# Latent attention: the units of the maximum pass end in step 18, and the maxima are turned ahead of the value group of step 20

## The chip, the cores and the metric

The program runs on one core of one Trainium2 chip. The metric is the device time of one execution in microseconds. Three runs of the kernel before are shown below; the profile is of one further execution.

## The reference, cut to what matters

Two layers of cross attention and feed-forward work on x (8 batches of 100 tokens, 256 wide). The change touches the attention of the second layer, which attends to a context of 1444 positions, 64 wide, for 16 heads:

```
scores = jnp.einsum('bhsr,bhlr->bhsl', q_r, k_r)
attn = jax.nn.softmax(scores, axis=-1)
ctx_c = jnp.einsum('bhsl,bld->bhsd', attn, kv_r)
ctx_lat = jnp.einsum('bhsd,hkd->bhsk', ctx_c, w_kc_kv)
x = x + jnp.tanh(g_xattn[1]) * (ctx_lat @ Wo.T)
```

The softmax subtracts the maximum over the 1444 positions from each row of scores. The kernel gets these maxima in a pass of its own, one batch ahead.

## The kernel before, in words

All of the attention of the second layer runs in one stage (ST_XB), with the order of the work written out by hand for each engine. For each of 8 batches there are 24 steps (SP_): 2 groups of 8 heads times 12 tiles of 121 context positions. The loops of TensorE, VectorE (DVE), ScalarE (ACT) and GpSimd (POOL) all count the same steps; semaphores hold them together.

In step s TensorE computes the scores of one tile: two matmuls with the high parts (L1748) and two with the low parts (L1751), 400 columns each. The second pair has 66 rows: 64 of the low part of the keys, and two rows of ones against which qm2 holds the negated maxima, as a high and a low part. So the maximum is subtracted inside the matmul, and scores(b, 0) waits until the DMA has written the maxima rows (semaphore qm). There are two pairs of PSUM banks for scores: step n waits for the exponential of step n - 2. ScalarE takes the exponential (L891) into a ring of 12 tiles, prob.

Every six steps (s % 6 == 2) TensorE does a value group (L1766): the values of six tiles times prob, accumulated in bank 7. The groups of batch b in steps 8, 14, 20 and in step 2 of the next batch; the one of step 20 reads steps 12 to 17 and needs nothing newer.

Between scores TensorE does the units of the maximum pass for batch b + 1 (queries_keys, L1730 and L1731): 39 units, 13 blocks of 128 rows by 3 segments of about 482 keys. VectorE takes the maximum of each unit out of PSUM (L1219). The table UNITS says how many units are done before step s. Units, the sums of probabilities (L1775), the projection (L1784) and the turned maxima share three banks in rotation (next_slot): a use waits until the third use before it has been emptied.

When the 39 units are done, VectorE reduces them to the negated maxima nmx (L1224, negative_maxima), TensorE turns nmx (L1737, maxima_turned), VectorE copies its high part nmh and low part nml out of PSUM (L1232, L1234, maxima_rows), and SyncE issues four DMAs (L447, L448) that write them into the two rows of qm2 for the next batch. On TensorE this turn is the last thing of step 20, behind the value group. On VectorE step 20 holds, in this order, the addition add_probabilities (L1242), negative_maxima and maxima_rows:

```
if s in (8, KT + 8) and b < B:
    add_probabilities(2 * b + s // KT, 8)
...
if s == 20 and more:
    negative_maxima(b + 1, k)
    maxima_rows(b + 1)
```

VectorE does more in these steps: four reciprocals of the sums (L1256, steps 16 to 19, behind the maxima of the step), the normalising of the context (L1261, step 19), in steps 0 and 1 of the next batch the last additions of the sums (L1247, L1251; the latter waits for the GpSimd addition of step 22), in step 2 the low parts of the next keys (low_keys, L1212, three of them), for which units of step 3 wait, and from step 3 again maxima. GpSimd adds the other tiles of probabilities (L658, L661) and rotates the keys of the batch after the next (L610, L612, L615).

slot_sums works out from UNITS at which use of the rotating banks the sums lie, so it follows the table.

Of the kernel before, what the change touches and what calls it, by code (L numbers as in the profile page):

```python
# [18 lines left out]
def flamingo(nc, a, out, scratch, sorted_x, sorted_y):  # L19
# [41 lines left out]
    with ctx:  # L61
# [216 lines left out]
        def end_stage(eng, turn):  # L278

            eng.drain().then_inc(stage, 1)  # L280
            eng.wait_ge(stage, turn * ENG)
# [12 lines left out]

        SP_ = 2 * KT
        NU = 3 * MT
        UNITS = (0, 0, 0, 0, 2, 4, 6, 8, 11, 14, 16, 18, 21, 24, 26, 29, 30, 32, 34, 36, 39, 39, 39, 39, 39)
        ADDS = (1, 1, 2, None, 3, 4, 5, None, 6, 7, 8, None)

        def key_rows(t):  # L300
# [6 lines left out]
        def slot_sums(i):  # L307

            p, late = (i + 1) // 2, i % 2 == 0
            first = NU + 1 + (0 if p == 0 else NU + 2 + (p - 1) * (NU + 4) - (0 if p < B else NU + 1))  # L310
            units = UNITS[KT + 4 if late else 4] if p + 1 < B else 0
            return first + units + (2 if late and p >= 1 else 0)

        def unit_columns(m):
            return slice(m * P, m * P + P) if m < MT - 1 else slice(HQ - P, HQ)
# [679 lines left out]
        def _(dve):  # L995
# [219 lines left out]
            def maximum(u):  # L1215

                k, g, m = next(slot), u // MT, u % MT
                dve.wait_ge(xb["fill"], k + 1)
                dve.tensor_reduce(mx3[:, m, g:g + 1], PS[:, 4 + k % 3, 0:SEG[g][1]], AX.X, ALU.max).then_inc(xb["free"], 1)  # L1219
                return next(freed)  # L1220
# [59 lines left out]
            for b in range(B + 1):  # L1280
                for s in range(SP_ if b < B else 11):
# [4 lines left out]
                    if more:  # L1286
                        for u in range(UNITS[s], UNITS[s + 1]):
                            k = maximum(u)
# [113 lines left out]
        def _(pe):  # L1402
# [306 lines left out]
            def next_slot(emptied_by):  # L1709

                k = len(held)
                if k >= 3:
                    pe.wait_ge(*held[k - 3])
                held.append(emptied_by)
                return 4 + k % 3
# [3 lines left out]
            def queries_keys(b, u):  # L1719

                g, m = u // MT, u % MT
                cols, keys = unit_columns(m), slice(SEG[g][0], SEG[g][0] + SEG[g][1])
                if m == 0:
                    pe.wait_ge(xb["kth"], 3 * b + g + 1)
                    pe.wait_ge(xb["kl"], 3 * b + g + 1)
                if u == 0:
                    pe.wait_ge(xb["one"], 1)
                    pe.wait_ge(xb["q2"], b + 1)
                bank = PS[:, next_slot((xb["free"], next(freed))), 0:SEG[g][1]]
                mm(bank, qs[:, b].rearrange("p h s -> p (h s)")[:, cols], kth[:, b % 2, keys], start=True, stop=False)  # L1730
                mm(bank, qm2[:, b % 2, cols], kl2[:, b % 2, keys], start=False, stop=True).then_inc(xb["fill"], 1)  # L1731

            def maxima_turned(b):

                k = next_slot((xb["free"], next(freed)))
                pe.wait_ge(xb["nmx"], b + 1)
                pe.transpose(PS[0:MT, k, 0:P], nmx[:], ident[:]).then_inc(xb["fill"], 1)  # L1737

            def scores(b, s):

                n, hp, t = b * SP_ + s, s // KT, s % KT
                keys = slice(t * KP, t * KP + key_rows(t))
                if s == 0:
                    pe.wait_ge(xb["qm"], 64 * (b + 1))
                if n >= 2:
                    pe.wait_ge(xb["ex"], n - 1)
                for g in range(2):
                    mm(PS[0:key_rows(t), 2 * (n % 2) + g, 0:GC], kth[:, b % 2, keys],  # L1748
                       qs[:, b, 8 * hp + 4 * g:8 * hp + 4 * g + 4].rearrange("p h s -> p (h s)"), start=True, stop=False)
                for g in range(2):  # L1750
                    last = mm(PS[0:key_rows(t), 2 * (n % 2) + g, 0:GC], kl2[:, b % 2, keys],  # L1751
                              qm2[:, b % 2, (2 * hp + g) * GC:(2 * hp + g + 1) * GC], start=False, stop=True)
                last.then_inc(xb["s"], 1)

            def values(c):

                b, i = c // 4, c // 2
                if c % 4 == 0:
                    pe.wait_ge(xb["nrot"], 3 * (b + 1))
                if c % 2 == 0 and i >= 1:  # L1760
                    pe.wait_ge(xb["raw"], i)
                pe.wait_ge(xb["ex"], 6 * c + 6)
                for n in range(6 * c, 6 * c + 6):
                    t = n % KT
                    for g in range(2):
                        last = mm(PS[g * DC:g * DC + DC, 7, 0:GC], kvn[0:key_rows(t), b % 2, t], prob[0:key_rows(t), n % RING, g],  # L1766
                                  start=(t == 0), stop=(t == KT - 1))
                last.then_inc(xb["pv"], 1)

            def probability_sums(i):  # L1770

                k = next_slot((xb["sums"], i + 1))
                pe.wait_ge(xb["ad"], 3 * i + 3)
                for g in range(2):
                    last = mm(PS[g * DC:g * DC + DC, k, 0:GC], ones[:], accd[:, g], start=True, stop=True)  # L1775
                last.then_inc(xb["fill"], 1)

            def project(b):

                k = next_slot((xb["free"], next(freed)))  # L1780
                pe.wait_ge(xb["cx"], 2 * b + 2)
                for c in range(NC):
                    for p in range(H1 // 2):
                        last = mm(PS[:, k, c * S:(c + 1) * S], w2p[:, p, c * P:(c + 1) * P], cx[:, p], start=(p == 0), stop=(p == H1 // 2 - 1))  # L1784
                last.then_inc(xb["fill"], 1)
# [3 lines left out]
            for b in range(B + 1):  # L1789
                for s in range(SP_ if b < B else 11):  # L1790
                    n, more = b * SP_ + s, b + 1 < B
                    if b < B:
                        scores(b, s)
                    if more:
                        for u in range(UNITS[s], UNITS[s + 1]):
                            queries_keys(b + 1, u)
                    if s % 6 == 2 and 8 <= n < B * SP_ + 3:
                        values((n - 8) // 6)
                    if s == 3 and b >= 1:
                        probability_sums(2 * b - 1)  # L1800
                    if s == KT + 3:
                        probability_sums(2 * b)
                    if s == 10 and b >= 1:
                        project(b - 1)
                    if s == 20 and more:
                        maxima_turned(b + 1)
            end_stage(pe, ST_XB)
            norm("n3", xT)
            end_stage(pe, ST_N3)
# [167 lines left out]
```

## Time and profile before

| | us |
|---|---|
| median of 3 runs | 1738.02 |
| the three runs | 1728.39, 1738.02, 1741.69 |
| the profiled execution | 1731.37 |
| its span | 1729.6 |
| TensorE (PE) busy | 1516.6 (88%) |
| VectorE (DVE) busy | 913.5 (53%) |
| ScalarE (ACT) busy | 592.5 (34%) |
| GpSimd (POOL) busy | 719.9 (42%) |
| mean granted TensorE clock | 0.92 |

The span is the time from the first to the last instruction of the profiled execution. The busy shares are means over all stages; the stage of the change takes some 500 us of the span, and what bounds it is to be read from its own stretches. A wait in brackets is the idle time of the engine ahead of an instruction and what ended it.

### The profile page before, as it was taken

Reading aid. Unit: us, or ns where it says so; the run is one execution under the profiler, and the core shown is the slowest. Engines: PE = TensorE matmul, PEld = TensorE weight load, DVE = VectorE, ACT = ScalarE, POOL = GpSimd, SP = SyncE. Lnnn points to the kernel's source line nnn. Section 1 sums busy time; section 2 is a strip of 40 time slices with the busy share of each in tenths; the row PEclk is TensorE's granted clock in tenths of the full one; section 3 lists DMA queues with packets and bytes.
Section 4 is the critical chain, followed back from the end, with each engine's and each line's share of the span. In section 5 each row is a group of like instructions: output and inputs, shape, how many; then the busy total and the mean of one; then the engine's idle time right before and its main releaser. Section 6 shows DMA issues by size and latency. Waiting matters only on the chain. (4 is left out here: it accounts for less than half of the span.)

```text
span 1729.6 us, 19632 instructions
## 1 busy us (share of the span) xinstructions
PE 1516.6 (88%) x6852; PEld 1060.0 (61%) x6852; DVE 913.5 (53%) x1402; ACT 592.5 (34%) x945; POOL 719.9 (42%) x509
## 2 busy tenths in 40 slices
PE   5897798899978999999999977789797978599998
PEld 3675465444446667666667643465555555499997
DVE  3744111356675766767767435745647272444454
ACT  2322121123323433433433433434434332234343
POOL 2731002046646786787876630423323131133231
PEclk8988898599997999999999998989899989699999
DMA  7004112610001101101100020000000000334441
GB/s 277 1 1 154 32 40 67 190 37 22 1 35 52 53 1 52 53 1 52 53 1 18 1 74 2 25 1 24 24 24 24 24 0 3 93 115 126 118 124 47
DMA packets 60297, 88.33 MB, mean 51 GB/s; under 512 B 7557, under 2 KB 44613, under 8 KB 60231
## 3 DMA queue, kind: packets, MB, share of 16 engines
q1 hardware_dynamic: 59206, 85.82, 15.7%
q0 software_dynamic: 1024, 1.64, 0.3%
q8 instruction: 40, 0.66, 0.2%
q14 instruction: 27, 0.21, 0.0%
HBM read 81.92 MB, written 5.41 MB: 50 GB/s over the span
## 5 line engine op out<-in xcount | busy, mean ns | idle before, releaser
L661 POOL TENSOR_TENSOR xc<-xc,prob 121x800 f32<-121x800 f32 x112 | 230.9, 2061 | 70.4 <-ACT prob L891 62.2
L891 ACT ACTIVATE prob<-PS 121x800 f32<-121x800 f32 x192 | 159.3, 838 | 269.2 <-PE PS L1751 266.4
L1219 DVE TENSOR_REDUCE mx<-PS 128x1 f32<-128x482 f32 (+1 forms) x312 | 185.5, 644 | 76.5 <-PE PS L1731 75.7
L585 POOL TENSOR_TENSOR e_wl<-e_wf,e_wh 128x768 fp32r<-128x768 f32 x33 | 70.9, 2148 | 200.8 <-ACT e_wh L815 159.3
L683 POOL TENSOR_TENSOR q<-q,qt 128x400 f32<-128x400 f32 x64 | 66.0, 1031 | 211.5 <-DVE qt L1338 211.5
L1766 PE MATMUL PS<-prob,kvn 121*64 121x400 f32 (+1 forms) x768 | 141.3, 518 | 0.9 <-ACT prob L891 0.9
L1748 PE MATMUL PS<-qs,kth 128*121 128x400 f32 (+1 forms) x384 | 117.4, 389 | 21.0 <-DMA qm<-nml 18.3
L1730 PE MATMUL PS<-kth,qs 128*128 128x482 f32 (+1 forms) x312 | 126.1, 404 | 7.6 <-DVE kl L1212 5.8
L1731 PE MATMUL PS<-kl,qm 66*128 66x482 f32 (+1 forms) x312 | 121.8, 390 | 0.0
L547 POOL TENSOR_TENSOR p<-d,sm 100x800 f32<-100x800 f32 x48 | 73.1, 1522 | 114.3 <-DVE sm L1041 114.3
L1751 PE MATMUL PS<-qm,kl 66*121 66x400 f32 (+1 forms) x384 | 109.6, 369 | 0.0
L1748 PEld LDWEIGHTS PS<-qs,kth 128*121 128x121 f32 (+1 forms) x384 | 69.2, 198 | 60.3 <-DMA qm<-nml 20.9
L1766 PEld LDWEIGHTS PS<-prob,kvn 121*64 121x64 f32 (+1 forms) x768 | 53.8, 141 | 76.9 <-issue 72.8
L1160 DVE TENSOR_TENSOR e_aw<-e_sg,PS 128x400 f32<-128x400 f32 x64 | 36.6, 571 | 116.3 <-ACT e_sg L821 116.3
L1836 PE MATMUL PS<-h,wq 128*128 128x400 f32 x256 | 92.4, 512 | 5.3 <-DVE q L1334 4.4
L1622 PE MATMUL PS<-e_hh,e_wh 128*128 128x400 f32 x264 | 93.2, 353 | 2.7 <-POOL e_wl L585 2.7
L1872 PE MATMUL PS<-o,wo 128*128 128x400 f32 x256 | 90.8, 511 | 3.7 <-ACT o L967 3.7
L1861 PE MATMUL PS<-pt,vg 100*128 100x400 f32 x128 | 55.6, 561 | 41.8 <-ACT pt L745 29.7
L1623 PE MATMUL PS<-e_hl,e_wh 128*128 128x400 f32 x264 | 92.0, 348 | 0.0
L1624 PE MATMUL PS<-e_hh,e_wl 128*128 128x400 f32 x264 | 91.7, 347 | 0.0
L739 ACT ACTIVATE d<-d 100x800 f32<-100x800 f32 x48 | 41.8, 870 | 134.2 <-DVE d L1033 134.2
L633 POOL TENSOR_TENSOR rr<-rp 96x400 f32<-96x400 f32 x32 | 32.9, 1027 | 117.1 <-DVE rp L1196 117.1
(248 smaller groups left out, 3178.0 us busy)
## 6 DMA issues: line engine op xcount, KB each, us to landing
e_wb<-routing SPq DMA_DIRECT2D x32, 400.0 KB, 3.9
wgu<-in_L_ffn_gate_up_proj SPq DMA_DIRECT2D x8, 1024.0 KB, 14.3
krt<-in_ctx_T SPq DMA_DIRECT2D x8, 722.0 KB, 4.2
ksw<-in_ctx_Tswap SPq DMA_DIRECT2D x8, 722.0 KB, 5.9
wdn<-in_L_ffn_down_proj SPq DMA_DIRECT2D x8, 512.0 KB, 8.6
wq<-in_L_ffn_Wq SPq DMA_DIRECT2D x4, 1024.0 KB, 5.2
wo<-in_L_ffn_Wo SPq DMA_DIRECT2D x4, 1024.0 KB, 5.4
e_wf<-in_L_ffn_Wg SPq DMA_DIRECT2D x32, 128.0 KB, 2.1
```

Of the source, the lines that this page charges most:

```text
L661: pool.tensor_tensor(accp, accp, prob[:, n % RING], ALU.add).then_inc(xb["ap"], 1)
L891: act.activation(prob[0:k, n % RING], PS[0:k, 2 * (n % 2):2 * (n % 2) + 2, 0:GC], ACT.Exp).then_inc(xb["ex"], 1)
L1219: dve.tensor_reduce(mx3[:, m, g:g + 1], PS[:, 4 + k % 3, 0:SEG[g][1]], AX.X, ALU.max).then_inc(xb["free"], 1)
L1622: mm(out_, wh, mh, start=start, stop=False)
L1623: mm(out_, wh, ml, start=False, stop=False)
L1624: return mm(out_, wl, mh, start=False, stop=stop)
L1730: mm(bank, qs[:, b].rearrange("p h s -> p (h s)")[:, cols], kth[:, b % 2, keys], start=True, stop=False)
L1731: mm(bank, qm2[:, b % 2, cols], kl2[:, b % 2, keys], start=False, stop=True).then_inc(xb["fill"], 1)
L1748: mm(PS[0:key_rows(t), 2 * (n % 2) + g, 0:GC], kth[:, b % 2, keys], qs[:, b, 8 * hp + 4 * g:8 * hp + 4 * g + 4].rearrange("p h s -> p (h s ...
L1751: last = mm(PS[0:key_rows(t), 2 * (n % 2) + g, 0:GC], kl2[:, b % 2, keys], qm2[:, b % 2, (2 * hp + g) * GC:(2 * hp + g + 1) * GC], start=F ...
L1766: last = mm(PS[g * DC:g * DC + DC, 7, 0:GC], kvn[0:key_rows(t), b % 2, t], prob[0:key_rows(t), n % RING, g], start=(t == 0), stop=(t == KT ...
L1836: last_ = mm(PS[:, QBANK[n], 0:HALF], wq2[:, c, (n % HG) * P:(n % HG + 1) * P], h1[:, c, half(n // HG)], start=(c == 0), stop=(c == NC - 1))
```

## The change

The table UNITS is another one: 27, 30, 31, 33, 36 and 39 units are done before steps 14 to 19, where 26, 29, 30, 32, 34 and 36 were; the last unit is in step 18 and not in step 19. The total stays 39. And on TensorE maxima_turned of step 20 stands ahead of the value group of that step. VectorE's order is left as it is, but for the maxima, which follow the table.

```
-        UNITS = (0, 0, 0, 0, 2, 4, 6, 8, 11, 14, 16, 18, 21, 24, 26, 29, 30, 32, 34, 36, 39, 39, 39, 39, 39)
+        UNITS = (0, 0, 0, 0, 2, 4, 6, 8, 11, 14, 16, 18, 21, 24, 27, 30, 31, 33, 36, 39, 39, 39, 39, 39, 39)
...
                     if more:
                         for u in range(UNITS[s], UNITS[s + 1]):
                             queries_keys(b + 1, u)
+                    if s == 20 and more:
+                        maxima_turned(b + 1)
                     if s % 6 == 2 and 8 <= n < B * SP_ + 3:
                         values((n - 8) // 6)
...
                     if s == 10 and b >= 1:
                         project(b - 1)
-                    if s == 20 and more:
-                        maxima_turned(b + 1)
```

## Rows read from the trace of the kernel before

**Rows 1.** The page: busy time of each engine, share, instructions.
```profile
PE 1516.6 (88%) x6852; PEld 1060.0 (61%) x6852; DVE 913.5 (53%) x1402; ACT 592.5 (34%) x945; POOL 719.9 (42%) x509
```

**Rows 2.** The view of the tile nml: who waited for it (us, times).
```profile
  PE PS L1748: 18.3, 8
```

**Rows 3.** Windows between two turns: us, busy time by engine, PEclk, DMA, GB/s.
```profile
577.68:642.06 64.38, 61.60 (x312) 43.69 (x313) 44.02 (x63) 25.02 (x32) 49.35 (x29) 0.95 0.11 36
...
897.84:960.40 62.56, 60.20 (x311) 43.17 (x312) 44.22 (x63) 25.04 (x32) 41.60 (x22) 0.97 0.05 13
```

**Rows 4.** Timeline of TensorE, first boundary: start, us, instruction, [idle before <-releaser].
```profile
571.48 0.39 PE L1730 MATMUL PS<-kth,qs 128*128 128x480 f32 x1
...
571.92 0.53 PE L1748 MATMUL PS<-qs,kth 128*121 128x400 f32 x2
...
572.75 4.25 PE L1766 MATMUL PS<-prob,kvn 121*64 121x400 f32 x24
577.68 0.27 PE L1737 MATMUL PS<-ident,nmx 128*13 128x128 f32 x1 [0.68 <-DVE nmx L1224]
...
582.53 1.02 PE L1748 MATMUL PS<-qs,kth 128*121 128x400 f32 x2 [1.93 <-DMA qm<-nml]
583.35 0.87 PE L1751 MATMUL PS<-qm,kl 66*121 66x400 f32 x2
```

**Rows 5.** Windows of 1 us, first boundary; the granted clock is third from the end.
```profile
583.00:584.00 1.00, 1.00 (x4) 0.96 (x4) 0.53 (x1) 0.00 (x0) 1.00 (x1) 0.50 0.00 0
...
588.00:589.00 1.00, 1.00 (x6) 0.37 (x4) 0.72 (x1) 1.00 (x2) 1.00 (x1) 0.56 0.00 0
```

**Rows 6.** Timeline of TensorE, third boundary.
```profile
711.53 0.85 PE L1748 MATMUL PS<-qs,kth 128*121 128x400 f32 x2 [1.93 <-DMA qm<-nml]
...
715.46 4.25 PE L1766 MATMUL PS<-prob,kvn 121*64 121x400 f32 x24
```

**Rows 7.** Timeline of VectorE, first boundary.
```profile
566.41 1.22 DVE L1219 TENSOR_REDUCE mx<-PS 128x1 f32<-128x480 f32 x2 [1.53 <-PE PS L1731]
...
575.44 1.99 DVE L1242 TENSOR_TENSOR xc<-prob 121x800 f32<-121x800 f32 x1
577.35 0.18 DVE L1224 TENSOR_REDUCE nmx<-mx 128x13 f32<-128x39 f32 x1
```

**Rows 8.** Timeline of ScalarE, first boundary: the exponentials of steps 21 and 22.
```profile
578.72 1.57 ACT L891 ACTIVATE prob<-PS 121x800 f32<-121x800 f32 x2 [5.03 <-PE PS L1751]
```

**Rows 9.** Timeline of TensorE, the first scores of batch 0.
```profile
521.82 1.02 PE L1748 MATMUL PS<-qs,kth 128*121 128x400 f32 x2 [4.75 <-DMA qm<-nml]
```

**Rows 10.** Timeline of GpSimd, first boundary: the additions of steps 21 and 22.
```profile
579.63 1.89 POOL L661 TENSOR_TENSOR xc<-xc,prob 121x800 f32<-121x800 f32 x1 [0.44 <-ACT prob L891]
...
582.64 2.64 POOL L661 TENSOR_TENSOR xc<-xc,prob 121x800 f32<-121x800 f32 x1
```

**Rows 11.** Timeline of VectorE, first and fourth boundary: last addition, low keys.
```profile
585.32 1.99 DVE L1251 TENSOR_TENSOR xc<-xc 121x800 f32<-121x800 f32 x1 [1.79 <-POOL xc L661]
...
779.47 5.22 DVE L1212 TENSOR_TENSOR kl<-krt,kth 64x482 fp32r<-64x482 f32 x3 [0.16 <-ACT kth L868]
```

**Rows 12.** Timeline of TensorE, first boundary: scores of step 3, first unit of step 4.
```profile
592.01 0.63 PE L1748 MATMUL PS<-qs,kth 128*121 128x400 f32 x2
...
595.45 0.39 PE L1730 MATMUL PS<-kth,qs 128*128 128x482 f32 x1
```

**Rows 13.** Timeline of TensorE, sixth and seventh boundary.
```profile
897.84 0.27 PE L1737 MATMUL PS<-ident,nmx 128*13 128x128 f32 x1 [0.67 <-DVE nmx L1224]
...
914.25 0.39 PE L1730 MATMUL PS<-kth,qs 128*128 128x482 f32 x1
...
955.91 4.25 PE L1766 MATMUL PS<-prob,kvn 121*64 121x400 f32 x24
...
974.51 0.62 PE L1748 MATMUL PS<-qs,kth 128*121 128x400 f32 x2
```

**Rows 14.** Timeline of VectorE: the addition L1251 of step 13, GpSimd idle.
```profile
622.19 0.98 DVE L1251 TENSOR_TENSOR xc<-xc 121x800 f32<-121x800 f32 x1
```

More of the change, by code:

```diff
@@ L296, in flamingo @@
         NU = 3 * MT
-        UNITS = (0, 0, 0, 0, 2, 4, 6, 8, 11, 14, 16, 18, 21, 24, 26, 29, 30, 32, 34, 36, 39, 39, 39, 39, 39)
+        UNITS = (0, 0, 0, 0, 2, 4, 6, 8, 11, 14, 16, 18, 21, 24, 27, 30, 31, 33, 36, 39, 39, 39, 39, 39, 39)
         ADDS = (1, 1, 2, None, 3, 4, 5, None, 6, 7, 8, None)
@@ L1796, in _ @@
                             queries_keys(b + 1, u)
+                    if s == 20 and more:
+                        maxima_turned(b + 1)
                     if s % 6 == 2 and 8 <= n < B * SP_ + 3:
@@ L1804, in _ @@
                         project(b - 1)
-                    if s == 20 and more:
-                        maxima_turned(b + 1)
             end_stage(pe, ST_XB)
```

## The prediction

> **What bounds the kernel.** I read the page first. TensorE is busy 88% of the span, no other engine more than 53% [rows 1]. Its costly groups send the reader to line 1748, the scores, whose idle time ends mostly with the copy of the maxima rows; the view of the tile nml puts that at 18.3 us in 8 waits, one for each batch [rows 2]. The windows between two turns of the maxima show what a batch costs: six of them, 62.6 to 64.6 us, the first 64.38 with TensorE busy 61.60 of them, the last 62.56 with 60.20 [rows 3]. So TensorE bounds this stage and every microsecond that it waits at a boundary between batches is a microsecond of the kernel. There are 7 boundaries that the edit touches (the eighth turn, of batch 0, is ahead of the loop).
>
> The timeline of TensorE at the first boundary shows what the reader has to see [rows 4]. The value group of step 20 starts at 572.75. The turn of the maxima comes behind it at 577.68, after 0.68 us of idle time that the negated maxima end. Steps 21 to 23 follow at once; then 1.93 us of idle time for the DMA, and the first scores of the new batch at 582.53. From there the matmuls take twice as long (0.87 for a pair instead of 0.53). The slices say why: the granted clock was 0.50, that is 1.2 GHz, from 583 us on, and back at 2.4 GHz within the slice from 588, some 6.4 us after work resumed [rows 5]. What went ahead was mostly idle time. At the third boundary it was back by the value group at 715.46, 3.9 us after work resumed at 711.53 [rows 6].
>
> **What decides is VectorE.** Its timeline at the first boundary has no gap from 566.41 to 577.53: nine maxima, four reciprocals, the normalising, the addition of probabilities (L1242, 1.99 us), and only then the 0.18 us reduction that makes nmx [rows 7]. The value group on TensorE lies exactly beside the tail of this. It is the cover of the wait that the edit uncovers.
>
> **The parts.**
> (a) Unit table: 39 units before and after, so no work is added. One unit (two matmuls, 0.44 us from the starts in [rows 4]) goes from step 19 to step 13, ahead of the value group of step 14; within steps 16 to 19 the rest is pushed forward. At step 20 TensorE arrives at the same time. VectorE has 8 maxima instead of 9 behind the value group of step 14 (one less, 0.57), but that value group ends 0.44 later, so nmx comes 0.13 us earlier. Bounds: 0.57 earlier, or 0.2 later (a bank not yet free). I take 0.13.
> (b) The turn moves ahead of the value group. TensorE reaches it at 572.75 instead of 577.0, and nmx is there at 577.40, plus the 0.15 us that passes in [rows 4, 7] between nmx and the turn: idle 4.8 us. Behind the waiting turn on TensorE's queue are the 24 matmuls of the value group and all later scores; on ScalarE the exponentials of steps 21 on, on GpSimd the additions that need them. The value group then takes 4.25 us at full clock (572.75 to the start of the idle time at 577.00, [rows 4]). So, counted from the point V where the value group used to start, scores of step 21 begin at V + 4.80 + 0.03 + 4.25 = V + 9.08, instead of V + 4.95.
> (c) The DMA wait goes. The copy to the rows lands 4.85 us after the turn (577.68 to 582.53), and now 4.25 us of values and 2.7 us of scores stand between. SP's four DMAs are issued by the turn as before; its other loads are not moved against it. What is late next is ScalarE: exp of step 22 ends at scores 21 + 2.59 [rows 8], so step 24 can start at + 2.7, 25 at + 3.9, 26 at + 4.65 (0.84 us an exp, two in 1.57), the value group of step 2 at + 5.5, and it ends at + 9.75.
> (d) Slow clock. Idle for 4.8 us will bring the clock to 1.2 GHz as 1.93 us did: after the 4.75 us wait of batch 0 the first pair took the same 1.02 us as at 582.53 [rows 4, 9]. Work then resumes with the value group, 24 matmuls that nothing but TensorE limits. Low clock lasted 3.9 to 6.4 us after work resumed [rows 5, 6]; half of that is lost: 1.9 to 3.2, I take 2.55. What the clock costs before is inside the times I compare with.
> (e) VectorE's next chain. Before, the DMA wait gave GpSimd and VectorE time to catch up. The exp of step 21 lets GpSimd do an addition (1.89), a rotation and an addition (2.64) [rows 10], then VectorE adds (L1251, from scores 21 + 7.62, 1.99 us) and only then makes the low keys, three of them in up to 5.22 us, since GpSimd adds beside them [rows 11], then the first maxima. With 7.62 + 2.14 + 5.2 + 0.65 + 0.15, the first unit of step 4, which needs the bank of the first unit of step 3, can't start before scores 21 + 15.7. TensorE alone would be there at 9.75 + 3.44 (592.01 to 595.45, [rows 12]) = 13.2. Before, the same unit started 17.77, 18.01, 16.42, 16.93, 18.00 and 16.41 us after the turn (mean 17.26; the first 577.68 to 595.45, the last 897.84 to 914.25, [rows 4, 12, 13]), with this chain hidden in the wait and the slow clock. It holds at six boundaries; at the last there are no more low keys.
>
> **The sum.** At six boundaries, from V to that unit: after 9.08 + 2.55 + 15.7 = 27.3; before 4.92 + 17.26 = 22.2; + 5.1 each, 30.6. At the last (V to the end of the values of step 2): after 4.36 + 0.03 + 4.25 + 2.55 + 9.75 = 20.9; before 955.91 to 974.51 = 18.6 [rows 13]; + 2.3. Together + 32.9. The waits of (e), 2.6 us in two pieces, may lower the clock once more, at most 2.5 us each time; I add 2 in all. The profiled execution took 1731.37 us, its span 1729.6; 1731.4 + 34.9 = 1766. The median of the three runs shown, 1738.02, is 6.6 above that execution, so a median of after could as well be 1772. Forecast: **1767**.
>
> The Trainium skill, page "TensorE: Matmul & The Clock Gate", section "Why this matters for your kernels", asks only that no long idle gaps stand between bursts; by it the short, divided waits of (e) cost no clock, and the sum would be 1764. The rows don't side with it: a gap of 1.93 us was enough.
>
> **Rivals.**
> *A, faster.* nmx is ready when TensorE arrives, and the DMA is simply issued 4 us earlier. Then, per boundary, the 0.68 and the 1.93 us go, and the slow clock with them; with (e) as it is, V + 0.05 + 4.25 + 15.7 = 20.0 against 22.2, and at the last 14.0 against 18.6: 6 x 2.2 + 4.6 = 18 us, 1713; without (e), 15 more. For it: one unit less behind the last value group. Against it: 11.1 us of VectorE without a gap. The point at which it turns: nmx some 2.2 us after V (by 575.0 at the first boundary, not 577.4), less what the clock costs. Chance 5%.
> The Trainium skill, page "DMA: Bandwidth & Descriptors", section "Rules for kernel authors", has this rule: issue a DMA early, compute, wait late. It is what the edit does and would give this rival; it says nothing of the wait ahead of the issue.
> *B, little.* (e) is hidden again (GpSimd's later start takes away its collision with VectorE: L1251 takes 0.98 us alone, [rows 14], and the keys less too). Then six boundaries give 9.08 + 2.55 + 13.2 - 22.2 = + 2.6, the last + 2.3: 18 us, 1749, just on the limit of what can be told. Without any fall of the clock it would be nothing, 1731. Chance 17%.
> *C, far slower.* The forecast, and the divided wait lowers the clock at each boundary, on scores and units: 6 x 2.5 = 15 more, 1781. Chance 18%.
> *D, nothing:* the order on TensorE doesn't come out as written (a turn that was held by a bank, not by nmx). Against it stands the wait put down to nmx at the turn [rows 4]. 2%.
> The forecast itself has 58%.
>
> **Range and chances.** Low end: B with a clock cost of 2.0: 6 x 2.1 + 1.8 = 14, 1746. High end: C on the level of the median, 1786. One per cent (17 us) is about what a measurement of this kernel can tell from no change. Slower by over 1%: the forecast, C and half of B: 85%. Within: 10%. Faster: 5%.
>
> **What would show it.** (b): the turn's wait for nmx grows from 0.68 to about 4.8 us and the value group stands behind it. (c): no wait of line 1748 for nml but that of batch 0. (d): granted clock 0.50 in the slices with the value group of step 20, and pairs of scores at 0.53 from step 24. (e): new waits of line 1730 for kl and mx at steps 3 and 4. A batch costs 66 to 70 us between two turns. It is wrong if nmx comes within 2.2 us of V, or if a batch stays under 65.

## The result, and the profile after

The changed kernel takes 1784.46 us (median of four runs, 1775.99 to 1788.28), the kernel before 1737.3; the ratio is 1.027, with a 95% interval of 1.022 to 1.033. By the medians it is slower by 47 us; the two profiled executions (1731.37 and 1785.53) are 54 us apart, where 35 had been forecast. The time lies in the range, at its upper end: 17 us above the forecast of 1767 and 2 us below the end of the range.

The windows between turns, two of them. They answer to [rows 3]; the columns are the same.

```profile
583.21:654.91 71.70, 65.26 (x311) 45.07 (x312) 45.98 (x63) 24.86 (x32) 49.78 (x29) 0.90 0.09 32
...
941.64:1013.65 72.01, 65.19 (x312) 45.06 (x312) 46.12 (x63) 24.79 (x32) 43.18 (x23) 0.90 0.04 11
```

A batch costs 71.7 us (72.0 the last) where it cost 63.8 on the mean, and the granted clock is 0.90 where it was 0.95 to 0.97. TensorE stands idle for 6.4 of these 71.7 us (before 2.8 of 64.4), and is busy 3.7 us longer, with the same matmuls: that goes with the lower clock.

The view of the tile nml, as in [rows 2]: one wait is left where eight were, that of batch 0.

```profile
  PE PS L1748: 4.8, 1
```

The timeline of TensorE at the first boundary, which answers to [rows 4]:

```profile
578.24 0.54 PE L1748 MATMUL PS<-qs,kth 128*121 128x400 f32 x2
578.62 0.52 PE L1751 MATMUL PS<-qm,kl 66*121 66x400 f32 x2
583.21 0.37 PE L1737 MATMUL PS<-ident,nmx 128*13 128x128 f32 x1 [4.07 <-DVE nmx L1224]
583.51 7.05 PE L1766 MATMUL PS<-prob,kvn 121*64 121x400 f32 x24
590.49 0.62 PE L1748 MATMUL PS<-qs,kth 128*121 128x400 f32 x2
...
603.32 0.53 PE L1751 MATMUL PS<-qm,kl 66*121 66x400 f32 x2
605.91 0.48 PE L1730 MATMUL PS<-kth,qs 128*128 128x482 f32 x1 [2.06 <-DVE mx L1219]
...
608.11 0.87 PE L1751 MATMUL PS<-qm,kl 66*121 66x400 f32 x2
```

Three things stand there. The turn waits 4.07 us for nmx (0.68 before), and TensorE has nothing else to do in this time. The value group behind it takes 7.05 us, not 4.25. And in step 4, 15.4 us after the scores of step 21, a second wait of 2.06 us for a bank is new; behind it a pair of scores takes 0.87 us again.

The slices around both waits (granted clock third from the end) answer to [rows 5]:

```profile
581.00:582.00 1.00, 0.00 (x0) 0.00 (x0) 1.00 (x2) 0.00 (x0) 1.00 (x1) 1.00 0.00 0
582.00:583.00 1.00, 0.00 (x0) 0.00 (x0) 1.00 (x2) 0.00 (x0) 1.00 (x2) 0.69 0.00 0
583.00:584.00 1.00, 0.80 (x3) 0.39 (x5) 0.41 (x3) 0.00 (x0) 1.00 (x2) 0.50 0.00 0
...
589.00:590.00 1.00, 1.00 (x8) 0.42 (x6) 0.00 (x0) 0.00 (x0) 0.00 (x0) 0.90 0.00 0
...
605.00:606.00 1.00, 0.09 (x1) 0.10 (x1) 1.00 (x3) 0.00 (x0) 1.00 (x1) 1.00 0.00 0
606.00:607.00 1.00, 1.00 (x3) 0.70 (x4) 0.59 (x2) 0.00 (x0) 1.00 (x1) 0.63 0.67 110
...
613.00:614.00 1.00, 1.00 (x7) 0.96 (x6) 0.99 (x2) 0.00 (x0) 1.00 (x1) 0.95 0.63 175
```

The clock falls to 1.2 GHz during the first wait and is back only at the end of the value group; it falls once more right behind the second wait and is back in the slice from 613. The other five boundaries that are followed by units read the same: the unit that waits 2.03 to 2.07 us starts 22.6 to 22.7 us after the turn, and from it to the value group of step 8 it takes 11.5 us at each, 8.47 at each before.

VectorE at the first boundary, as in [rows 7]:

```profile
578.92 1.41 DVE L1256 RECIPROCAL sq<-sq 128x100 f32<-128x100 f32 x2
580.37 0.68 DVE L1261 TENSOR_TENSOR hT<-sq 128x400 f32<-128x400 f32 x1
580.97 1.98 DVE L1242 TENSOR_TENSOR xc<-prob 121x800 f32<-121x800 f32 x1
582.88 0.18 DVE L1224 TENSOR_REDUCE nmx<-mx 128x13 f32<-128x39 f32 x1
```

The reciprocals, the normalising and the addition stand between the last maximum (578.9) and nmx: 4 us in which TensorE has nothing to do. The turn comes 4.14 us after V (583.21 - 579.07, the end of the scores of step 20).

### The profile page after: what moved, and what is told of

Its sections match the earlier page's. It is cut to its first block and busy times, and to the rows that moved or that the text cites. A ratio compares the mean times of both kernels' runs of the same rounds, so it can differ in the third digit from the quotient of the medians.

```text
span 1783.8 us, 19632 instructions
## 1 busy us (share of the span) xinstructions
PE 1547.8 (87%) x6852; PEld 1071.4 (60%) x6852; DVE 921.0 (52%) x1402; ACT 591.3 (33%) x945; POOL 722.7 (41%) x509
## 5 line engine op out<-in xcount | busy, mean ns | idle before, releaser
L661 POOL TENSOR_TENSOR xc<-xc,prob 121x800 f32<-121x800 f32 x112 | 225.9, 2017 | 106.5 <-ACT prob L891 99.2
L1766 PE MATMUL PS<-prob,kvn 121*64 121x400 f32 (+1 forms) x768 | 155.4, 560 | 0.9 <-ACT prob L891 0.9
L1730 PE MATMUL PS<-kth,qs 128*128 128x482 f32 (+1 forms) x312 | 133.6, 428 | 20.2 <-DVE mx L1219 12.7
L1731 PE MATMUL PS<-kl,qm 66*128 66x482 f32 (+1 forms) x312 | 128.4, 412 | 0.0
L1766 PEld LDWEIGHTS PS<-prob,kvn 121*64 121x64 f32 (+1 forms) x768 | 58.1, 153 | 85.3 <-issue 83.4
L1730 PEld LDWEIGHTS PS<-kth,qs 128*128 128x128 f32 x312 | 64.3, 206 | 42.5 <-DVE mx L1219 27.5
```

What stands on the lines that cost most here:

```text
L661: pool.tensor_tensor(accp, accp, prob[:, n % RING], ALU.add).then_inc(xb["ap"], 1)
```

## The experiments

Each is measured side by side with the kernel before, on the same chip (two chips in all; the median of the kernel before lies between 1734.4 and 1734.9 us there). The changed kernel was not run again beside them. So where two variants are compared, the profiled executions, counted from turn to turn, are the surer measure.

**The table alone** (the new UNITS, the turn where it was).

> The unit table alone; the turn of the maxima stays behind the value group of step 20. Theory (the move of the turn does the harm, the table is neutral): nmx comes at most 0.2 us away from where it was, the waits for nmx (0.68 us) and for the DMA (1.93 us) stay, a batch costs 63 to 65 us between turns, ratio 0.995 to 1.005. Rival (pushing units ahead of the value group of step 14 makes VectorE late for the banks): 1 us or more a batch, ratio 1.005 or more.

Measured: 1736.97 us, ratio 1.000 (0.996 to 1.004). The timeline of TensorE at the first boundary:

```profile
572.75 4.25 PE L1766 MATMUL PS<-prob,kvn 121*64 121x400 f32 x24
576.93 0.28 PE L1737 MATMUL PS<-ident,nmx 128*13 128x128 f32 x1
581.79 0.64 PE L1748 MATMUL PS<-qs,kth 128*121 128x400 f32 x2 [1.94 <-DMA qm<-nml]
585.40 6.25 PE L1766 MATMUL PS<-prob,kvn 121*64 121x400 f32 x24
```

The wait for nmx behind the value group is gone, which I had expected to stay: the table brings nmx 0.76 us nearer to V (the start of the value group of step 20), not 0.13: its reduction starts at 576.59 here and at 577.35 before, with V at 572.75 in both. It buys nothing, since the DMA wait stays and the value group of step 2 now lies in the slow stretch (6.25 us; 5.2 to 6.8 at the seven boundaries).

**The turn alone** (the table of before).

> The move of the turn alone, with the unit table of before. Theory (what counts is VectorE's chain up to nmx, and the table shortens it by at most 0.6 us against the arrival of TensorE): the turn waits 4 to 5 us for nmx, the value group behind it takes about 7 us, a batch costs 71 to 73 us between turns, ratio 1.025 to 1.035. Rival (the table matters, since with three units in step 19 nmx is late by them): the turn waits 6 us or more, a batch 74 us, ratio 1.04.

Measured: 1775.6 us, ratio 1.022 (1.018 to 1.027), just under the stated bound. A batch costs 67.5 to 73.9 us and not 71 to 73. The turn waits 4.80 us at five boundaries, 6.81 at one and 4.40 at the last; at the one, the normalising on VectorE took 4.30 us and not 1.30:

```profile
576.82 0.37 PE L1737 MATMUL PS<-ident,nmx 128*13 128x128 f32 x1 [4.80 <-DVE nmx L1224]
577.12 6.64 PE L1766 MATMUL PS<-prob,kvn 121*64 121x400 f32 x24
```

So the move of the turn is the loss. With the longer wait it was no slower than the whole change: the median is 9 us lower, with intervals of the ratio that overlap, and the stage from the first turn to the last takes 477.8 us against 489.8. The second wait is there at all six boundaries (2.02 to 2.08 us), but the clock fell behind it at two only: from that unit to the value group of step 8 it took 11.5 and 12.7 us at these and 8.6 at the other four. A wait of 2 us can lower the clock and need not. The value group of step 20 took 5.6 to 6.6 us and not 7.05: by slices of 1 us the clock fell 0.3 to 4.5 us ahead of the turn here and 0.8 to 1.2 in the changed kernel, so that more of the slow stretch had passed when the value group came, or, at the one boundary with 0.3, the stretch was shorter (3.4 us).

**The wait filled.** Extra work, no part of the computation, ahead of the wait:

```diff
                 k = next_slot((xb["free"], next(freed)))
+                if b > 0:
+                    for _ in range(22):
+                        mm(PS[:, k, 0:GC], kth[:, (b + 1) % 2, 0:P], qs[:, b - 1, 0:4].rearrange("p h s -> p (h s)"), start=True, stop=True)
                 pe.wait_ge(xb["nmx"], b + 1)
```

> The changed kernel with 22 extra matmuls of 400 columns (about 4.0 us at full clock) ahead of the turn's wait for nmx, into the bank that the turn overwrites: TensorE works in the time in which it stood idle, and nothing else is moved. Theory (the idle time lowers the clock, and the slow clock is a cost of its own, 2.8 us a boundary in the value group): the value group takes 4.25 us in place of 7.05, 7 x 2.8 = 20 us less than the changed kernel, some 1765 us, ratio 1.016; the second wait of 2.06 us and the slow matmuls behind it stay. Rival (the value group is slow for what it reads beside GpSimd and VectorE, not by the clock): it stays at 7 us and the time stays at 1784, ratio 1.027.

Measured: 1764.8 us, ratio 1.017 (1.013 to 1.021). The timeline of TensorE at the first boundary:

```profile
578.11 4.19 PE L1738 MATMUL PS<-qs,kth 128*128 128x400 f32 x22
582.33 0.28 PE L1740 MATMUL PS<-ident,nmx 128*13 128x128 f32 x1
582.54 4.25 PE L1769 MATMUL PS<-prob,kvn 121*64 121x400 f32 x24
```

The turn comes as late as in the changed kernel (4.1 us after the scores), but the value group takes 4.25 us, and the granted clock is 1.00 from 577 to 601 us. TensorE does 22 matmuls more per boundary and the kernel is faster than the changed one, by 20 us of the medians and 17.6 of the profiled executions; the seven value groups give 20. That shows the clock as a cost of its own, apart from the wait. The second wait and the slow stretch behind it stayed at all six boundaries (11.3 to 12.8 us to the value group of step 8; the two of over 12 take back some of the 20).

**The third low keys later**, first try:

```diff
                     if s == 2 and more:
-                        for g in range(3):
+                        for g in range(2):
                             low_keys(b + 1, g)
...
+                    if s == 9 and more:
+                        low_keys(b + 1, 2)
```

> The changed kernel, but VectorE makes the third low part of the next keys in step 9 and not in step 2, so that the first maxima of a batch come about 2 us sooner. Theory (the second slow stretch comes from the 2.06 us wait for a bank in step 4): the wait shrinks under 0.5 us, the clock stays at 1.00 in steps 4 to 8, a batch costs about 66.6 us and not 71.7 (2.06 of waiting and 3.1 of slow clock gone), 6 x 5.1 = 31 us less, some 1754 us, ratio 1.009. Rival (the slow stretch follows from the long wait at the turn, whatever happens in step 4): only the 2 us of waiting go, 12 us, some 1772, ratio 1.020. Second rival (VectorE is late all through steps 3 to 8, and the wait only moves): ratio 1.025 or more.

Measured: 1813.0 us, ratio 1.044 (1.038 to 1.049): none of the three. The bank wait did go, and its clock; but SyncE issues the loads of the next values behind the wait for all three low keys, so they went from step 3 to step 9 as well. SyncE's timeline, and what GpSimd makes of it:

```profile
630.15 0.36 SPq L413 DMA_DIRECT2D krt<-in_ctx_T  x1
...
631.46 0.80 SPq L418 DMA_DIRECT2D rstd<-in_ctx_Nswap  x1
```

```profile
640.13 1.84 POOL L623 TENSOR_TENSOR rstd<-rstd,ksinN 121x768 f32<-121x768 f32 x1 [18.71 <-DMA rstd<-in_ctx_Nswap]
```

GpSimd stood for 18.71 us on this load, and for 18.4 to 20.3 us at the next four boundaries; in the changed kernel it had waited for it 2.3 us in all. Its additions, which free the ring of exponentials, stand behind that instruction in its order. The queue that I had not followed was SyncE's.

**The same with the values loaded first.**

```diff
             for b in range(-1, B):
-                if b + 2 < B:
-                    sp.wait_ge(xb["kl"], 3 * (b + 2))
-                    load_turned(b + 2)
                 if 0 <= b < B - 1:
...
                     load_values(b + 1)
+                if b + 2 < B:
+                    sp.wait_ge(xb["kl"], 3 * (b + 2))
+                    load_turned(b + 2)
```

> As third_keys_later, but on SyncE the values of the next batch are loaded ahead of its turned keys, so that they no longer queue behind the wait for the third low keys. Theory (the slow stretch in steps 4 to 7 comes from the 2.06 us wait for a bank, and third_keys_later was slow only since the values came 20 us late): a batch costs 66.6 us and not 71.7, 31 us less than the changed kernel, some 1754 us, ratio 1.009. Rival (the later keys make something else late too, the loads of the turned keys above all, which GpSimd rotates from step 12): a batch of 70 us or more, ratio 1.022 or more.

Measured: 1746.69 us, ratio 1.007 (1.004 to 1.009). The turn's wait is as it was, no bank wait is left in step 4, and a batch costs

```profile
580.29:645.96 65.67, 61.31 (x312) 42.14 (x312) 43.02 (x63) 24.90 (x32) 50.13 (x29) 0.97 0.10 35
908.32:973.91 65.59, 60.94 (x312) 42.11 (x312) 43.36 (x63) 24.94 (x32) 43.48 (x23) 0.97 0.05 12
```

5.6 to 6.7 us less than with the change, 6.1 on the mean. Beside the 2.06 of waiting and the 3.1 of slow clock (8.5 us to the value group of step 8 at all six), the value group of step 20 was somewhat faster here, 5.6 to 6.7 us. The first rival of the run before, that the second slow stretch follows from the wait at the turn, is out: that wait is the same here, and the clock stayed at 1.00 in steps 4 to 8.

**The same in the kernel before.**

> The kernel before with only the third low keys in step 9 and the values loaded first. Theory (before the change VectorE's chain behind the turn was hidden by the DMA wait and the slow clock): no bank wait to take away, a batch stays at 63 to 65 us, ratio 0.995 to 1.003. Rival (the later keys are a gain by themselves): ratio 0.99 or less.

Measured: 1734.05 us, ratio 1.000 (0.997 to 1.002). So before the change this chain cost nothing that can be measured.

**The reduction in step 18**, on the changed kernel:

```diff
                             k = maximum(u)
+                    if s == 18 and more:
+                        negative_maxima(b + 1, k)
+                    if s == 20 and more:
+                        maxima_rows(b + 1)
...
-                    if s == 20 and more:
-                        negative_maxima(b + 1, k)
-                        maxima_rows(b + 1)
```

> The changed kernel, with VectorE reducing the maxima right behind the last unit in step 18, ahead of two reciprocals, the normalising and the addition, and copying the turned maxima at the head of step 20. Theory (the loss is the wait for nmx, and nothing in the move itself): the turn waits 0.3 us or less, the value group takes 4.25 us, scores of step 21 start 4.4 us behind V; the wait of 2.06 us in step 4 and the slow stretch behind it stay, 3.1 us. V to the first unit of step 4 is 19.8 us (before 22.2), from there to the next V 44.9 (before 41.7): + 0.8 at six boundaries, - 4.4 at the last, about 1737 us, ratio 1.000. Rival (the DMA wait of the maxima rows comes back, since VectorE copies them only behind its reciprocals and the normalising): 1 us or more a boundary and the clock with it, ratio 1.01.

Measured: 1734.53 us, ratio 0.999 (0.997 to 1.001). The timeline of TensorE:

```profile
579.35 0.27 PE L1738 MATMUL PS<-ident,nmx 128*13 128x128 f32 x1 [0.24 <-DVE nmx L1224]
579.54 4.25 PE L1767 MATMUL PS<-prob,kvn 121*64 121x400 f32 x24
...
599.46 0.77 PE L1731 MATMUL PS<-kth,qs 128*128 128x482 f32 x1 [2.19 <-DVE mx L1219]
```

The first wait and its clock are gone and with them the whole loss; what the DMA gives is eaten by the second wait, 2.13 to 2.19 us at six boundaries, and by the clock, which fell behind it at four of them (10.1 to 12.8 us to the value group of step 8, 8.6 at the other two).

**Both.** The reduction in step 18, the third low keys in step 9, the values loaded first.

> Both: the reduction in step 18, and the third low keys in step 9 with the values loaded first. Theory (the two waits that the change opened, and the clock behind each, are all of its loss): V to the first unit of step 4 17.7 us, from there to the next V 41.7, a batch 59.4 us against 63.8 before, 6 x 4.4 + 4.4 = 31 us less than before, some 1705 us, ratio 0.982. Rival (VectorE is then the bound in steps 3 to 8 and 16 to 20, as its queue has no slack left): a batch of 62 us or more, ratio 0.993 or more.

Measured: 1707.75 us, ratio 0.984 (0.980 to 0.988). It is 27 us faster than the kernel before, which its interval clears.

```profile
580.97:641.09 60.12, 59.56 (x311) 41.61 (x312) 42.63 (x64) 24.99 (x33) 50.16 (x29) 1.00 0.12 38
641.09:701.20 60.11, 59.60 (x312) 41.55 (x312) 42.61 (x64) 24.98 (x33) 50.94 (x29) 1.00 0.12 38
```

TensorE is busy 59.6 of 60.1 us and the clock of these windows is 1.00 (so it is in all six).

**Both, with the turn behind the value group again.**

> reduce_and_keys, but with the turn behind the value group again, as before the change. It tells whether the gain needs the move of the turn or comes from the earlier reduction and keys alone. Theory (the move is what hides the DMA of the maxima rows): nmx waits for TensorE, the 0.68 us go, but the wait of 1.9 us for the DMA and the slow clock behind it are back, a batch 63 us, some 1728 us, ratio 0.996. Rival (the gain comes from VectorE's order): ratio 0.985.

Measured: 1736.26 us, ratio 1.000 (0.999 to 1.003). The DMA wait is back, and even the 0.68 us bought nothing:

```profile
588.10 0.62 PE L1751 MATMUL PS<-qs,kth 128*121 128x400 f32 x2 [1.95 <-DMA qm<-nml]
591.75 6.19 PE L1769 MATMUL PS<-prob,kvn 121*64 121x400 f32 x24
```

The first scores behind the wait are still at full clock, and the slow stretch lies over the value group of step 2 (5.3 to 6.8 us), whose matmuls wait for nothing else. A batch costs 64.1 to 65.4 us, 63 had been expected. So the gain of the run before needs the move of the turn: it is a good idea that lacked its condition.

**Both, with the table of before** (the reduction in step 19).

> reduce_and_keys with the unit table of before; the reduction then stands behind the last unit in step 19. Theory (the table is worth what the last maxima come later than V: in the trace of before the three of step 19 end 0.7 us after V, with nmx at + 0.9): the turn waits about 1.1 us instead of 0.25, 0.9 us more a batch at seven boundaries, no slow clock, ratio 0.987 to 0.989. Rival (1.1 us is enough to lower the clock in the value group): 2 us more a boundary, ratio 0.995.

Measured: 1712.8 us, ratio 0.987 (0.983 to 0.990). The turn waits 1.00 to 1.02 us, the value group takes 4.25, and the clock stayed at 1.00: a wait of 1.0 us didn't lower it. The turn waits 0.76 us longer than in reduce_and_keys, but most of that isn't in the time: four of the six batches are 0.3 us longer (60.4 for 60.1), the mean of six 0.5, the stage from the first turn to the last 3.4 (420.3 for 416.8). The medians differ by 5 us, with intervals that overlap. So the table is worth 3.4 us by the stage and 5 by the medians, which these runs don't tell from nothing for sure.

## Why the prediction was right, and where its terms were off

The sign and the mechanism of the first wait were right. That the time lies in the range is in part luck: its upper end came from rival C, which is what happened, and the forecast itself was 17 us short.

**(a) and (b), the wait for nmx.** Right in kind: V to the turn is 4.14 us, 4.80 was forecast. It was mis-sized because I moved VectorE's chain as a block with its durations. The normalising starts 0.14 us nearer to V, as forecast (V + 1.29; V + 1.43 before). But it takes 0.68 us here and took 1.33 before (at 574.18, in the gap of [rows 7]). GpSimd works beside it in both kernels; what makes the difference was not tested. At the last boundary it takes 2.02 us, and V to the turn is 4.47, 4.36 in the forecast. Together 0.65 x 6 - 0.1 = 3.8 us less than forecast.

**(c), the DMA wait.** Right: gone at all seven boundaries. ScalarE paced the scores behind it as worked out (0.18 us of waiting for the exponential at 592.43); from the scores of step 21 to the value group of step 2 it was 5.58 us (596.07 - 590.49), 5.5 in the forecast.

**(d), the slow clock.** Right, shown by the filled wait. 2.8 us a boundary for 2.55 (2.6 at the last).

**(e), VectorE's next chain.** Right: scores of step 21 to the first unit of step 4 took 15.42 us, 15.7 was forecast and 13.2 without the chain. VectorE's timeline has the chain that was forecast:

```profile
598.17 1.99 DVE L1251 TENSOR_TENSOR xc<-xc 121x800 f32<-121x800 f32 x1 [1.79 <-POOL xc L661]
600.08 5.20 DVE L1212 TENSOR_TENSOR kl<-krt,kth 64x482 fp32r<-64x482 f32 x3
605.21 1.21 DVE L1219 TENSOR_REDUCE mx<-PS 128x1 f32<-128x482 f32 x2
```

The first of these two maxima frees the bank that the unit at 605.91 waits for. The third low keys, moved to step 9, took the wait with them.

**The failed term** is "the waits of (e), 2.6 us in two pieces, may lower the clock once more ...; I add 2 in all". The wait came in one piece of 2.06 us, because the first low keys were there in time and the first unit of step 3 did not wait. In the changed kernel that lowered the clock at every one of six boundaries. From that unit to the next V it took 44.9 us (from 605.91, turn + 22.7, to the next V at turn + 67.6), 41.7 before: 3.2 us each, 19.1 in all where 2 had been put. That is rival C, with 18% of the chances, at 3.2 a boundary and not 2.5. That it fell at all six is not a rule: the same wait did it at six of six in filled_wait, four of six in reduce_in_18 and two of six in turn_alone. In the changed kernel the batches are alike to 0.06 us (71.65 to 71.71, the last apart), so what happened at one boundary happened at all; why it was the bad case is not shown. With it the sum closes: 32.9 - 3.8 (a, b) + 2.9 (d and the start of the value group, 0.44 x 6 + 0.27) - 1.8 (e) + 19.1 = 49.3 us. The traces have 49.6 between the first V and the end of the last boundary's value group of step 2 (1030.53 - 579.07 = 451.46, 974.59 - 572.75 = 401.84 before). The 54 us between the two profiled executions are these, 7.1 us by which the first turn of all comes later, ahead of anything that the change touches, and small differences the other way.

**The rivals.** A turned on nmx coming within 2.2 us of V. The reduction in step 18 made that true (0.24 us) and the time was 1734.5: with (e) and the clock behind it still there, none of the forecast 18 us was left. Without (e) it was 1707.75, 27 us under the kernel before, where A's 18 and the 15 more without (e) make 33. B asked for (e) to be hidden again, which keys_later_values_first forces: 12 us over the kernel before in the same rounds, 18 in the forecast. D is out: the turn's wait is put down to nmx, and moving the reduction ended it.

By the rule of the Trainium skill, page "TensorE: Matmul & The Clock Gate", section "Why this matters for your kernels", which speaks of long gaps only, the 2.06 us wait would have cost no clock; the slices show that the clock fell behind it. The rule to issue a DMA early (the Trainium skill, page "DMA: Bandwidth & Descriptors", section "Rules for kernel authors") pays here once nmx is early too (reduce_and_keys); alone, following it cost 47 us.

## What to carry to other kernels

Before an instruction that waits is moved ahead of one that doesn't, follow the chain that ends its wait back on the other engine, instruction by instruction: what it is moved ahead of is the cover of that chain (here a value group that was ready and stood 4.07 us behind the turn). Move the producer forward first (here a 0.18 us reduction, ahead of some 4 us of reciprocals, normalising and addition that it doesn't need), then the waiting instruction. And price a wait on TensorE as the wait plus the slow stretch that can follow it: here 4.1 + 2.8 and 2.06 + 3.2 us. And before a step is put off, look what stands behind it on the queue that waits for it: SyncE's wait for the third low keys held back loads that didn't need them.

## What the runs showed of the hardware that I had not expected

A wait of about 2.1 us cost up to 4.3 us behind it, twice itself, or nothing: over the four kernels that have it in step 4 the clock fell after 18 of 24. A wait of 1.0 us at the turn (both_old_table) never cost more than itself. What a slow stretch costs hangs on what lies under it: 2.8 us over the value group, whose matmuls nothing else limits (7.05 for 4.25 us), and 3.1 over the units and scores of steps 4 to 7 (11.5 for 8.5 us). Over the scores of steps 24 to 26 alone, which ScalarE paces, it was 0.8 us or a little more: in the kernel before, the value group of step 2 began 9.1 us after the turn at the four boundaries where all of them lay in the slow stretch, and 8.3 at the one where the clock fell 1.8 us behind the start of the first.

Filling the waits at the turn with matmuls that compute nothing made the kernel 18 to 20 us faster (profiled executions, medians).

Ahead of this stage, in code that no kernel here changes, the profiled executions differ by more than some verdicts: the first turn stands at 516.8 us in the kernel before, 523.9 in the changed one, 516.7 in turn_alone and 525.2 in reduce_and_keys. What causes that was not looked into; windows counted from the turns leave it out.
